# A Mamba-2 mixer with a mixture of experts: the count table stored step by step, the carry moved into a limit, the shared weights split during the mixer

## The chip, the cores and the metric

The kernel runs on one core of one Trainium2 chip. A core has a matrix engine (PE, with its weight loads shown apart as PEld), a vector engine (DVE), a scalar engine (ACT), GpSimd (POOL) and a sync engine (SP) that only issues DMAs. The engines run their own instruction lists and meet at semaphores. The metric is device time in microseconds, the median of several runs; lower is better. Everything is fp32.

## The reference

One block of a network over x of shape (2, 4096, 256), in two halves.

```
x = x + layernorm(mamba2(layernorm(x)))                  # the mixer
x = x + layernorm(moe(layernorm(x)))                     # the experts

moe(x):   T = 8192 tokens, E = 64 experts, top 8, capacity 128
  gu     = x @ shared_gate_up_w                          # (256, 1024)
  shared = silu(gu[:, :512]) * gu[:, 512:] @ shared_down_w
  shared = shared * sigmoid(x @ shared_gate_w)
  w, idx = top_k(softmax(x @ gate_w), 8);  w /= sum(w)
  pos    = how many earlier (token, choice) pairs took the same expert
  buf[e, slot] = x[token]     for slot = pos < 128
  out_e  = (silu(buf @ gate) * (buf @ up)) @ down        # per expert, 128 slots
  y      = sum over the token's choices of w * out_e[e, slot], 0 if pos >= 128
  return y + shared
```

Only the first 128 tokens (in order) that choose an expert reach it. So the kernel needs, per expert, a running count of choices over the 8192 tokens, and for each expert and slot 0..127 the token that sits there.

## The kernel before

**Mixer.** 32 steps; a step treats 128 tokens of both batches. The function `iteration(i)` of each engine is a software pipeline of depth 5: at `i` it works on parts of steps i, i-1, ... i-4 (`j0` to `j4`, and `j5`). Steps 0 to 6 and the last 8 are written out, the middle is a hardware loop. The order of the instructions on each engine is fixed by hand in these functions. In part `j4` PE multiplies the chosen-matrix by a triangle of ones into bank 1, and DVE adds the count so far (`count_now`, L1021) and writes 128 columns of `counts`, a tile of 128 partitions (64 experts times two batches) by 32 x 128 tokens; the two batches are counted apart. At `i + 1` DVE copies the last column into `count_now` (L830). SP loads x three steps ahead, stores the normed rows and router weights into the token table (L441, L446) and the transposed normed rows (L436). After three x loads SP also issues the zero fill of `routed_sum` (L423, L425). POOL starts each iteration with the small operations of the layernorm scale (L1034, then a power on L1027), and every tensor-tensor operation of POOL carries L1027, every one of DVE L807, every plain copy of ACT L665 here and L1523 in the experts' stage.

**Between the stages.** All engines wait for the mixer's stores, meet at a barrier, and SP clears the semaphores. The experts' stage then starts with a head. ACT issues the loads of the shared weights (L1525, L1526). PE moves the final count of batch 0 to the partitions of batch 1 (the carry); DVE keeps it (L1698), adds it to the 32 counts at step ends (L1700, `ends`), and compares those with 1..128 (`ends_before`, L1705, two halves); PE sums the comparisons (L1395), which gives for each expert and slot the step ("chunk") in which its token lies; DVE turns this into row numbers of the count table (L1709 to L1712). ACT adds the carry to the whole of `counts` (L1530), and only then SP stores it as the count table in HBM (L1261), with one row of 1..128 more (L1264). ACT writes a high part of the shared weights (L1532, L1534), DVE the rest (L1715, L1717), since the fp32 products there are made of three products of split parts. ACT and DVE wait for the table store before the loop.

**Experts' loop.** `iteration_r1` runs 16 rounds and drains: each round gathers count rows for four experts (POOL, indirect DMA, L1965 to L1983), compares them with `slot` (L1780 and on), which gives the token, gathers the tokens' rows, runs the experts, and adds the results into `routed_sum` by indirect DMA; in between PE makes the shared part from `xt` tiles that SP loads (L1275), ACT and DVE split (L1761, L1764). `row_now` holds the four row numbers of a round and is filled in two halves (L1738, L1767).

```
eng.wait_ge(carry_ready, 1)
eng.wait_ge(ends_kept, 1)
nc.scalar.activation(counts[:, :], counts[:, :], ACT.Identity, bias=carry).then_inc(counts_total, 1)
```

## Time and profile before

| | us |
|---|---|
| median of 3 runs | 1413.08 (1411.3 to 1415.54) |
| profiled execution, its own time | 1406.39 |
| span of its trace | 1404.7 |
| PE busy | 1225.8 (87%) |
| DVE busy | 1035.7 (74%) |
| POOL busy | 908.1 (65%) |
| ACT busy | 866.9 (62%) |

The span reaches from the first to the last instruction; 1.69 us of the execution lie around it. Busy shares are means over stages with different limits: the mixer until about 925, the head until about 946, the experts' loop and a last part that adds, normalises and stores.

### The profile page before, as it was taken

The numbers are of one execution on the slowest core, as the hardware profiler recorded it, in microseconds if no ns is written. First come the engines' busy times: TensorE is split into PE (matmuls) and PEld (weight loads), VectorE is DVE, ScalarE is ACT, GpSimd is POOL, SyncE is SP. The second block draws the span as 40 slices with busy tenths as digits, with TensorE's granted clock in tenths as the row PEclk, the third lists the DMA queues.
The fourth block names the chain that finished last, engine by engine and source line by source line (L and its number), as shares of the span: only waits on it lengthen the run. The fifth ranks groups of instructions, "written<-read, shape, count | busy, mean of one in ns | idle before, by whom it ended". The sixth has DMA issues, their size and how long they took to land. (4 is left out here: it accounts for less than half of the span.)

```text
span 1404.7 us, 27142 instructions
## 1 busy us (share of the span) xinstructions
PE 1225.8 (87%) x8578; PEld 1070.5 (76%) x8578; DVE 1035.7 (74%) x3118; ACT 866.9 (62%) x1882; POOL 908.1 (65%) x1049
## 2 busy tenths in 40 slices
PE   2899999999999999999999999729998999998960
PEld 2778778778777877877877787519998999998950
DVE  3789989998998999999899899544344344443894
ACT  2677777777777777777777777434444344444453
POOL 0466677667667767766766776516667677663586
PEclk9899999999999999999999999859999999999985
DMA  5600010011001001001100000156766676764565
GB/s 159 198 7 25 26 42 33 24 34 39 24 26 40 31 24 41 32 24 34 39 24 26 34 23 18 44 165 161 183 176 155 169 181 163 168 161 99 188 203 171
DMA packets 112935, 119.90 MB, mean 85 GB/s; under 512 B 19889, under 2 KB 99057, under 8 KB 112881
## 3 DMA queue, kind: packets, MB, share of 16 engines
q1 hardware_dynamic: 97744, 94.58, 21.4%
q0 software_dynamic: 14336, 23.08, 8.7%
q10 hardware_dynamic: 800, 1.57, 0.3%
q8 instruction: 27, 0.44, 0.1%
q14 instruction: 28, 0.22, 0.1%
HBM read 70.63 MB, written 48.56 MB: 85 GB/s over the span
## 5 line engine op out<-in xcount | busy, mean ns | idle before, releaser
L1027 POOL TENSOR_TENSOR mamba_arena<-mamba_arena 128x512 f32<-128x512 f32 (+2 forms) x384 | 383.3, 1009 | 245.0 <-DVE mamba_arena L807 199.4
L456 PE MATMUL bank<-identity,mamba_arena 128*128 128x128 f32 x704 | 112.5, 279 | 53.1 <-DVE mamba_arena L916 27.4
L807 DVE TENSOR_TENSOR mamba_arena<-bank,mamba_arena 128x512 f32<-128x512 f32 (+1 forms) x224 | 136.4, 610 | 15.9 <-PE bank L500 10.0
L456 PEld LDWEIGHTS bank<-identity,mamba_arena 128*128 128x128 f32 x704 | 85.0, 146 | 80.2 <-issue 27.2
L1378 PE MATMUL bank<-xt_hi,wsgu_hi 128*128 128x256 f32 x384 | 114.0, 297 | 17.2 <-DVE xt_lo L1761 13.8
L1378 PE MATMUL bank<-xt_lo,wsgu_hi 128*128 128x256 f32 x384 | 109.6, 285 | 0.0
L1378 PE MATMUL bank<-xt_hi,wsgu_lo 128*128 128x256 f32 x384 | 109.6, 285 | 0.0
L665 ACT ACTIVATE mamba_arena<-bank 128x512 f32<-128x512 f32 x192 | 100.4, 540 | 9.0 <-PE bank L456 6.6
L1378 PEld LDWEIGHTS bank<-xt_hi,wsgu_hi 128*128 128x128 f32 x384 | 74.6, 194 | 18.8 <-DVE xt_lo L1761 14.5
L807 DVE TENSOR_TENSOR mamba_arena<-bank_s,mamba_arena 128x1024 f32<-128x1024 f32 x64 | 77.9, 1217 | 3.5 <-ACT bank_s L705 2.2
L669 ACT ACTIVATE mamba_arena<-x_all,mamba_arena 128x256 f32 (+1 forms) x128 | 69.5, 594 | 12.1 <-DVE mamba_arena L853 7.3
L1378 PEld LDWEIGHTS bank<-xt_lo,wsgu_hi 128*128 128x128 f32 x384 | 74.6, 194 | 0.4
L1378 PEld LDWEIGHTS bank<-xt_hi,wsgu_lo 128*128 128x128 f32 x384 | 74.5, 194 | 0.0
L1027 POOL TENSOR_TENSOR mamba_arena<-mamba_arena,minus_half 128x2 f32<-128x2 f32 x96 | 68.4, 712 | 7.8
L596 PEld LDWEIGHTS bank<-mamba_arena 128*128 128x128 f32 x256 | 47.0, 193 | 30.7 <-ACT mamba_arena L757 17.8
L596 PE MATMUL bank<-mamba_arena 128*128 128x256 f32 x256 | 65.1, 398 | 0.6
L478 PEld LDWEIGHTS bank<-mamba_arena 128*128 128x128 f32 x256 | 48.5, 190 | 20.0 <-issue 14.9
L1027 POOL TENSOR_TENSOR run_moving<-run_t,head_of 64x1024 fp32r<-64x1024 f32 x32 | 60.6, 1892 | 4.4 <-ACT run_t L665 4.4
L565 PE MATMUL bank<-mamba_arena 128*128 128x64 f32 x512 | 60.8, 272 | 0.5 <-DVE mamba_arena L807 0.5
L500 PE MATMUL bank<-mamba_arena 128*128 128x64 f32 x512 | 61.0, 272 | 0.1
L478 PE MATMUL bank<-mamba_arena 128*128 128x256 f32 x256 | 60.6, 379 | 0.0
L565 PEld LDWEIGHTS bank<-mamba_arena 128*128 128x128 f32 x512 | 59.7, 192 | 0.7 <-DVE mamba_arena L807 0.7
(368 smaller groups left out, 4479.1 us busy)
## 6 DMA issues: line engine op xcount, KB each, us to landing
experts_arena<-in_egu SPq DMA_DIRECT2D x64, 256.0 KB, 3.7
routed_sum<-zeros SPq DMA_DIRECT2D x1, 8320.0 KB, 27.0
x_all<-in_x SPq DMA_DIRECT2D x32, 256.0 KB, 2.7
token_table<-mamba_arena SPq DMA_DIRECT2D x64, 128.0 KB, 1.7
normed_transposed<-mamba_arena SPq DMA_DIRECT2D x32, 256.0 KB, 2.1
experts_arena<-normed_transposed SPq DMA_DIRECT2D x32, 256.0 KB, 3.8
experts_arena<-in_edown SPq DMA_DIRECT2D x64, 128.0 KB, 3.0
experts_arena<-routed_sum SPq DMA_DIRECT2D x32, 256.0 KB, 3.4
```

Source lines behind the costliest of these rows:

```text
L456: return nc.tensor.transpose(out, in_, identity[:, :])
L478: last = nc.tensor.matmul(bank[0][:, 1 * DM:2 * DM], yt[:, 1, c, :], w_out[:, c, :], start=c == 0, stop=c == KI - 1)
L500: last = nc.tensor.matmul(bank[5][:, h * HD:(h + 1) * HD], decay[:, 0, h, :], xdt[:, 0, h, :], start=True, stop=True)
L565: last = nc.tensor.matmul(bank[2][:, h * HD:(h + 1) * HD], decay[:, 1, h, :], xdt[:, 1, h, :], start=True, stop=True)
L596: last = nc.tensor.matmul(bank[0][:, 0 * DM:1 * DM], yt[:, 0, c, :], w_out[:, c, :], start=c == 0, stop=c == KI - 1)
L665: return nc.scalar.activation(out, in_, ACT.Copy)
L669: last = nc.scalar.activation(out[:, b, :], x[b], ACT.Identity, bias=shift[:, b:b + 1], scale=scale[:, b:b + 1])
L807: return nc.vector.tensor_tensor(out, a, b, op)
L1027: return nc.gpsimd.tensor_tensor(out, a, b, op)
L1378: last = nc.tensor.matmul(out[:, f * 256:(f + 1) * 256], w[:, k, columns], x[:, k, :], start=n == 0, stop=n == len(parts) - 1)
```

## The change

Six edits.

1. `counts` shrinks to one step (128 x 128). Each step's counts go to the count table as soon as DVE has written them: SP issues two DMAs of 64 rows at the end of its iteration, behind the router weights. DVE waits, before it writes the next step's counts, for that store and for a copy of the last column that POOL now makes into `ends` (its first instruction of every iteration from i = 5).
2. The table therefore holds batch 1 without the carry. The comparison `count + carry <= slot` becomes `count <= slot - carry`: DVE computes once `limit`, per slot and expert, with the carry taken off where the chunk lies in batch 1 (four more small operations; PE adds one product that spreads the carries over the partitions), and each round copies four columns into `limit_now`.
3. The head loses ACT's addition over `counts`, the two large table stores and the waits on them.
4. The shared weights are loaded by SP in the mixer, behind the first three x loads and ahead of the zero fill, into slots of `x_all` that are used later. ACT writes the high part in six pieces of 128 x 512 in iterations 0 to 5 (the first waits for both loads), POOL subtracts for the rest in iterations 1 to 6.
5. `row_now` is filled at once, for round 0 already in the head.
6. `silu_s` and `act_s` get tiles of their own, since `counts` no longer has room for them.

```diff
-        counts = sb("counts", [P, STEPS * P])
+        counts = sb("counts", [P, P])
+        ends = sb("ends", [P, STEPS])
...
# SP, mixer
+                eng.dma_start(wsgu_raw, sgu_d.rearrange("(k p) f -> p k f", p=P)).then_inc(wsgu_loaded, 16)
+                eng.dma_start(wsdown_raw, sdown_d.rearrange("(k p) f -> p k f", p=P)).then_inc(wsdown_loaded, 16)
                 rows = (TOK + CAP) // P
...
+                    if real(j4):
+                        eng.wait_ge(counts_ready, j4 + 1)
+                        eng.nop(nofuse=True)
+                        for b in range(NB):
+                            eng.dma_start(counts_d[bass.ds(j4 * NE + b * STEPS * NE, NE), :], counts[b * NE:(b + 1) * NE, :]).then_inc(counts_stored, 16)
                 pipeline(eng, iteration)
+                eng.wait_ge(counts_stored, 32 * STEPS)
...
# ACT, mixer, behind the squares
+                    if is_number(i) and i < 6:
+                        if i == 0:
+                            eng.wait_ge(wsgu_loaded, 16)
+                            eng.wait_ge(wsdown_loaded, 16)
+                        copy(shared_piece(wsgu_hi, wsdown_hi, i), shared_piece(wsgu_raw, wsdown_raw, i)).then_inc(shared_high, 1)
...
# DVE, mixer
+                        if real(j4 - 1):
+                            eng.wait_ge(counts_stored, 32 * j4)
+                            eng.wait_ge(end_kept, j4)
+                        nc.vector.tensor_scalar(counts[:, :], bank[1][:, 0:P], count_now[:, :], None, ALU.add).then_inc(counts_ready, 1)
...
# POOL, mixer
+                    if real(j5):
+                        eng.wait_ge(counts_ready, j5 + 1)
+                        eng.nop(nofuse=True)
+                        nc.gpsimd.tensor_copy(ends[:, bass.ds(j5, 1)], counts[:, P - 1:P]).then_inc(end_kept, 1)
...
+                    if is_number(i) and 0 < i < 7:
+                        eng.wait_ge(shared_high, i)
+                        tt(shared_piece(wsgu_lo, wsdown_lo, i - 1), shared_piece(wsgu_raw, wsdown_raw, i - 1),
+                           plain(shared_piece(wsgu_hi, wsdown_hi, i - 1)), ALU.subtract)
...
# SP, experts
-                eng.wait_ge(counts_total, 1)
-                for b in range(NB):
-                    eng.dma_start(counts_v[:, b * STEPS:(b + 1) * STEPS, :],
-                                  counts[b * NE:(b + 1) * NE, :].rearrange("e (i t) -> e i t", t=P)).then_inc(tables_out, 16)
...
# ACT, experts
-                nc.scalar.activation(counts[:, :], counts[:, :], ACT.Identity, bias=carry).then_inc(counts_total, 1)
-                eng.wait_ge(wsgu_loaded, 16)
-                nc.scalar.activation(wsgu_hi[:, :, :], wsgu_raw, ACT.Copy).then_inc(sgu_split[0], 1)
-                eng.wait_ge(wsdown_loaded, 16)
-                nc.scalar.activation(wsdown_hi[:, :, :], wsdown_raw, ACT.Copy).then_inc(sdown_split[0], 1)
-                eng.wait_ge(tables_out, 16 * 3)
...
# DVE, experts, head and round
+                nc.vector.scalar_tensor_tensor(row_of[:, :], chunk_of, float(NE), expert, ALU.mult, ALU.add).then_inc(row_ready, 1)
+                eng.wait_ge(row_ready, 1)
+                nc.vector.tensor_copy(row_now[:, :], row_of[:, 0:4]).then_inc(row_now_ready, 1)
...
+                nc.vector.tensor_tensor(limit, late, spread_bank, ALU.mult).then_inc(late_carry, 1)
+                eng.wait_ge(late_carry, 1)
+                nc.vector.tensor_scalar(limit, limit, -1.0, slot, ALU.mult, ALU.add).then_inc(limit_ready, 1)
...
-                        nc.vector.tensor_scalar(below[:, 0, 0, :], slot_counts[:, 0, 0, :], slot, None, ALU.is_le, ALU.add,
+                        nc.vector.tensor_scalar(below[:, 0, 0, :], slot_counts[:, 0, 0, :], limit_now[:, 0:1], None, ALU.is_le, ALU.add,
```

The first place is DVE in the head, from the sum of the comparisons to the first split of an `xt` tile. In brackets stand the semaphores waited for; those of the last rows bear names of the mixer, whose numbers they reuse. Before:

```order
L1709 COPY experts_arena<-bank 128x64 [waits chunks_counted]
L1711 TENSOR_SCALAR experts_arena<-experts_arena 128x64 [waits chunks_kept]
L1712 SCALAR_TENSOR_TENSOR row_of<-experts_arena 128x64
L1715 TENSOR_TENSOR wsgu_lo<-experts_arena,wsgu_hi 128x2048 [waits sgu_split0]
L1717 TENSOR_TENSOR wsdown_lo<-experts_arena,wsdown_hi 128x1024 [waits sdown_split0]
L1738 COPY row_now<-row_of 128x2 [waits row_ready,tables_out]
L1761 TENSOR_TENSOR xt_lo<-experts_arena,xt_hi 128x512 [waits o_scale]
```

And in the changed kernel:

```order
L1725 COPY experts_arena<-bank 128x64 [waits chunks_counted]
L1727 SCALAR_TENSOR_TENSOR row_of<-experts_arena 128x64 [waits chunks_kept]
L1729 COPY row_now<-row_of 128x4 [waits row_ready]
L1730 TENSOR_SCALAR experts_arena<-experts_arena 128x64
L1731 TENSOR_SCALAR experts_arena<-experts_arena 128x64
L1733 SCALAR_TENSOR_TENSOR experts_arena<-experts_arena 128x64 [waits late_from]
L1735 TENSOR_TENSOR experts_arena<-experts_arena,bank 128x64 [waits late_only]
L1737 TENSOR_SCALAR experts_arena<-experts_arena 128x64 [waits late_carry]
L1758 COPY experts_arena<-experts_arena 128x4 [waits limit_ready]
L1781 TENSOR_TENSOR xt_lo<-experts_arena,xt_hi 128x512 [waits x2_ready]
```

The two wide subtractions and the wait on the table are gone; `row_now` stands two operations behind the sum, and five small operations on 64 columns and a copy stand before the split.

The second place is SP in the mixer's loop, from the rows' store to the loop's end, before:

```order
L441 ISA [waits x2_normed]
L441 DMA token_table<-mamba_arena 128x256
L441 ISA
L441 DMA token_table<-mamba_arena 128x256
L446 ISA [waits weights_ready]
L446 DMA token_table<-mamba_arena 128x64
L446 ISA
L446 DMA token_table<-mamba_arena 128x64
L406 REGISTER_ALU
L406 COMPARE_AND_BRANCH
```

And the end of the same loop in the changed kernel:

```order
L460 ISA [waits weights_ready]
L460 DMA token_table<-mamba_arena 128x64
L460 ISA
L460 DMA token_table<-mamba_arena 128x64
L465 ISA [waits counts_ready]
L465 DMA count_table<-counts 64x128
L465 ISA
L465 DMA count_table<-counts 64x128
L418 REGISTER_ALU
L418 COMPARE_AND_BRANCH
```

Two issues and a wait on DVE are added behind the last store of the iteration, ahead of the next x load.

The third is the start of POOL's loop, in the changed kernel:

```order
L1062 ISA [waits counts_ready]
L1062 COPY ends<-counts 128x1
L1064 REGISTER_ALU
L1066 TENSOR_SCALAR mamba_arena<-mamba_arena 128x2 [waits x_mean]
L1055 TENSOR_TENSOR mamba_arena<-mamba_arena,minus_half 128x2 [waits x_var]
```

The last two rows are those with which the loop began before; the first three are new.

## Rows read from the trace of the kernel before

**Rows 1.** Stretches: us, busy PE, PEld, DVE, ACT, POOL, PE clock, DMA share, GB/s.
```profile
422.00:827.00 405.00, 385.43 (x2564) 320.11 (x2563) 369.34 (x1066) 301.18 (x631) 281.66 (x360) 1.00 0.09 31
925.00:944.00 19.00, 2.65 (x34) 2.25 (x34) 9.29 (x13) 7.74 (x4) 0.48 (x3) 0.50 0.81 211
```

**Rows 2.** Chain that ended last, over the head: start, us, what.
```profile
925.30 0.43 ACTq L1525
...
927.58 3.72 ACT counts L1530
...
931.31 0.66 SPq L1261
...
932.03 2.33 SPq L1261
...
934.41 5.08 SPq L1264
...
939.52 5.18 DMA experts_arena<-normed_transposed
```

**Rows 3.** DVE's timeline in the head: start, us, instruction [idle before, releaser].
```profile
926.78 4.49 DVE L1705 TENSOR_TENSOR experts_arena<-experts_arena 128x2048 bf16<-128x2048 f32 x2
932.40 0.23 DVE L1709 COPY experts_arena<-bank 128x64 f32<-128x64 f32 x1 [1.13 <-PE bank L1395]
...
932.77 0.22 DVE L1712 SCALAR_TENSOR_TENSOR row_of<-experts_arena 128x64 uint32<-128x64 f32 x1
```

**Rows 4.** Timeline of all engines at the start of the loop.
```profile
943.91 0.17 DVE L1738 COPY row_now<-row_of 128x2 uint32<-128x2 uint32 x1 [7.37 <-issue]
...
944.79 0.63 ACT L1523 ACTIVATE xt_hi<-experts_arena 128x512 fp32r<-128x512 f32 x1 [10.76 <-DMA experts_arena<-normed_transposed]
944.98 1.24 POOL L1965 DMA_INDIRECT experts_arena<-count_table,row_now  x1 [19.17 <-DVE row_now L1738]
945.45 0.69 DVE L1761 TENSOR_TENSOR xt_lo<-experts_arena,xt_hi 128x512 fp32r<-128x512 f32 x1 [1.37 <-ACT xt_hi L1523]
```

**Rows 5.** SP's timeline: the last issue of the mixer.
```profile
922.37 0.81 SPq L446 DMA_DIRECT2D token_table<-mamba_arena  x2
```

**Rows 6.** Timeline of all engines in the drain, iteration 34.
```profile
910.59 0.32 DVE L1021 TENSOR_SCALAR counts<-bank,count_now 128x128 f32<-128x128 f32 x1
910.83 0.22 POOL L1042 TENSOR_SCALAR mamba_arena<-mamba_arena 128x2 f32<-128x2 f32 x1 [0.61 <-DVE mamba_arena L1013]
...
912.13 1.09 ACT L669 ACTIVATE mamba_arena<-x_all,mamba_arena 128x256 f32<-128x256 f32 x2 [3.23 <-DVE mamba_arena L853]
```

**Rows 7.** Timeline of all engines in iteration 0.
```profile
25.66 0.62 SPq L423 DMA_DIRECT2D routed_sum<-zeros  x1
...
31.67 0.22 ACT L720 ACTIVATE mamba_arena<-mamba_arena 128x16 f32<-128x16 f32 x1 [1.29 <-DVE mamba_arena L903]
...
32.34 0.16 DVE L911 TENSOR_SCALAR mamba_arena<-mamba_arena 128x16 f32<-128x16 f32 x1
```

**Rows 8.** DMA issues: count, KB each, median us from issue to landing.
```profile
count_table<-counts SPq DMA_DIRECT2D x2, 1024.0 KB, 9.0
...
experts_arena<-in_sdown ACTq DMA_DIRECT2D x1, 512.0 KB, 6.1
```

**Rows 9.** DVE's waits from 400 to 805: us in total, times, longest.
```profile
DVE xnt_lo L807 <- ACT xnt_hi L665: 11.1, 15, 0.8
...
DVE mamba_arena L849 <- PE bank L478: 3.7, 15, 0.3
```

**Rows 10.** Timeline at the turn of two iterations of the mixer's loop.
```profile
420.50 1.04 POOL L1027 TENSOR_TENSOR mamba_arena<-mamba_arena 128x512 f32<-128x512 f32 x1 [1.17 <-DVE mamba_arena L807]
...
421.61 0.66 DVE L807 TENSOR_TENSOR mamba_arena<-mamba_arena 128x512 f32<-128x512 f32 x1
421.86 0.49 POOL L1034 TENSOR_SCALAR mamba_arena<-mamba_arena 128x2 f32<-128x2 f32 x1 [0.31 <-DVE mamba_arena L821]
```

**Rows 11.** POOL's timeline, iteration 3, at the place of a new piece.
```profile
104.50 1.29 POOL L1027 TENSOR_TENSOR mamba_arena<-mamba_arena 128x512 f32<-128x512 f32 x1 [1.00 <-DVE mamba_arena L807]
```

More of the change, by code:

```diff
@@ L105, in build @@
         x_all = sb("x_all", [P, NB, STEPS, DM])
-        counts = sb("counts", [P, STEPS * P])
+        counts = sb("counts", [P, P])
+        ends = sb("ends", [P, STEPS])
+        wsgu_hi, wsgu_lo = (sb(f"wsgu_{part}", [P, KD, 2 * FS], F32R) for part in ("hi", "lo"))
+        wsdown_hi, wsdown_lo = (sb(f"wsdown_{part}", [P, FS // P, DM], F32R) for part in ("hi", "lo"))
         shared_tanh = sb("shared_tanh", [P, NB, STEPS])
@@ L392, in real, with shared_piece @@
             return not is_number(j) or 0 <= j < STEPS
+        def shared_piece(gate_up, down, c):
+            return gate_up[:, c // 2, (c % 2) * FS:(c % 2 + 1) * FS] if c < 4 else down[:, 2 * (c - 4):2 * (c - 4) + 2, :].rearrange("p k d -> p (k d)")
         def draining(i):
@@ L829, in iteration @@
                         eng.nop(nofuse=True)
-                        nc.vector.tensor_copy(count_now[:, :], counts[:, bass.ds(j5 * P + (P - 1), 1)])
+                        nc.vector.tensor_copy(count_now[:, :], counts[:, P - 1:P])
                     if real(j1):
@@ L1125, in build @@
         shared = view(NB, STEPS // 2, DM)
-        wsgu_raw = shared[:, 1, 0:KD * 2 * FS // DM, :].rearrange("p (k a) d -> p k (a d)", k=KD)
-        wsdown_raw = shared[:, 1, KD * 2 * FS // DM:][:, 0:FS // P, :]
-        ends = view(STEPS)
+        carry_spread, late = shared[:, 1, 0, 0:NE], shared[:, 1, 0, NE:2 * NE]
         ends_before = (shared[:, 0, 0:STEPS * P // (2 * DM), :].rearrange("p a d -> p (a d)").bitcast(BF16)
@@ L1137, in build @@
         slot = view(1)
+        limit = view(NE)
+        limit_now = view(2 * 2)
         expert = view(NE)
@@ L1394, in _ @@
                         eng.wait_ge(ends_compared, 1 if i == 0 else 2)
-                    last = nc.tensor.matmul(chunk_bank[:, 0:NE], ends_before[:, i, :], fold, start=i == 0, stop=i == STEPS - 1)
+                    last = nc.tensor.matmul(chunk_bank, ends_before[:, i, :], fold, start=i == 0, stop=i == STEPS - 1)
                 last.then_inc(chunks_counted, 1)
@@ L1694, in _ @@
                 nc.vector.memset(carry_from[:, 0:NE], 0.0)
-                nc.vector.tensor_copy(carry_from[:, NE:P], identity[:, 0:NE]).then_inc(carry_matrix, 1)
+                nc.vector.tensor_copy(carry_from[:, NE:P], identity[:, 0:NE])
+                nc.vector.tensor_scalar(carry_spread[0:NE, :], identity[0:NE, 0:NE], count_now[0:NE, :], None, ALU.mult).then_inc(carry_matrix, 1)
                 nc.vector.tensor_tensor(fold, identity[:, 0:NE], identity[:, NE:P], ALU.add)
                 eng.wait_ge(carry_moved, 1)
-                nc.vector.tensor_copy(carry, carry_bank[:, 0:1]).then_inc(carry_ready, 1)
+                nc.vector.tensor_copy(carry, carry_bank).then_inc(carry_ready, 1)
                 eng.wait_ge(carry_ready, 1)
-                nc.vector.tensor_scalar(ends, counts[:, P - 1::P], carry, None, ALU.add).then_inc(ends_kept, 1)
+                nc.vector.tensor_scalar(ends[:, :], ends[:, :], carry, None, ALU.add).then_inc(ends_kept, 1)
                 eng.wait_ge(ends_kept, 1)
@@ L1737, in iteration_r1 @@
                         eng.nop(nofuse=True)
-                        nc.vector.tensor_copy(row_now[:, 0, :], row_of[:, bass.ds(4 * j0 + 0, 2)]).then_inc(row_now0, 1)
+                        if not is_number(j0) or j0 > 0:
+                            nc.vector.tensor_copy(row_now[:, :], row_of[:, bass.ds(4 * j0, 4)]).then_inc(row_now_ready, 1)
+                        nc.vector.tensor_copy(limit_now, limit[:, bass.ds(4 * j0, 4)]).then_inc(limits_now, 1)
                     if real(j1, 16):
@@ L1783, in iteration_r1 @@
                         eng.wait_ge(counts_gathered01, 16 * j0 + 16)
-                        nc.vector.tensor_scalar(below[:, 0, 1, :], slot_counts[:, 0, 1, :], slot, None, ALU.is_le, ALU.add,
+                        nc.vector.tensor_scalar(below[:, 0, 1, :], slot_counts[:, 0, 1, :], limit_now[:, 1:2], None, ALU.is_le, ALU.add,
                                                 accum_out=offset[:, 0, 1:2]).then_inc(offset_ready01, 1)
@@ L1806, in iteration_r1 @@
                         eng.wait_ge(counts_gathered10, 16 * j0 + 16)
-                        nc.vector.tensor_scalar(below[:, 1, 0, :], slot_counts[:, 1, 0, :], slot, None, ALU.is_le, ALU.add,
+                        nc.vector.tensor_scalar(below[:, 1, 0, :], slot_counts[:, 1, 0, :], limit_now[:, 2:3], None, ALU.is_le, ALU.add,
                                                 accum_out=offset[:, 1, 0:1])
@@ L1810, in iteration_r1 @@
                         eng.wait_ge(counts_gathered11, 16 * j0 + 16)
-                        nc.vector.tensor_scalar(below[:, 1, 1, :], slot_counts[:, 1, 1, :], slot, None, ALU.is_le, ALU.add,
+                        nc.vector.tensor_scalar(below[:, 1, 1, :], slot_counts[:, 1, 1, :], limit_now[:, 3:4], None, ALU.is_le, ALU.add,
                                                 accum_out=offset[:, 1, 1:2]).then_inc(offset_ready11, 1)
```

70 lines of the change are left out of this document (29 added, 41 removed).

## The prediction

> **What bounds the kernel now.** I read the stretches first, to see which stage has a hole. In the mixer's loop PE is busy for 385 of 405 us at full clock: a bound by PE, with DVE close behind, where little can be won. Between 925 and 944 PE is busy for 2.65 of 19 us and its granted clock is at the lower level, 0.50 [rows 1]. Then the chain of waits, to see what holds that hole open: ACT's pass over `counts` (3.72 us), two table stores on SP's queue (0.66 and 2.33), the small store behind them, which sits 5.08 in a full queue, and then the load of the first `xt` tile, 5.18 [rows 2]. Last the timelines of the single engines there: DVE is done with the row numbers at 932.99 (932.77 + 0.22) and fills `row_now` only at 943.91 [rows 3, 4], held by the wait on the table. So one chain, count table first and everything else behind it, sets the start of the experts' loop. The shared weights are not what ends last.
>
> **The head of the experts' stage.** I count from its start, 925.30 [rows 2], and call that 0. Before, the two events that start the loop are POOL's first gather of count rows at 19.7 (944.98) and the end of the first split of `xt` at 20.8 (945.45 + 0.69) [rows 4].
>
> Removed from that chain: 3.72 + 0.66 + 2.33 + 5.08 = 11.8 us of it. What is late next is DVE. It begins its comparisons at 1.5, they take 4.49 and PE's sum ends at 7.1, where DVE copies it (932.40) [rows 3]; none of this changes, but for one small operation and one small product ahead of it, which I set at 0.1. Then:
> - copy 0.23 and row numbers 0.22 end at 7.65, the fill of `row_now` (0.17) at 7.8. POOL began its gather 0.9 after that copy's end before (944.08 to 944.98) [rows 3, 4], so now at 8.7: 11.0 earlier.
> - the rest of `limit` and the copies are six operations, each about 0.22 by the row-number operation and partly waiting for its forerunner: 1.3 us, so DVE is free at 9.1. The `xt` tile is issued by SP behind one small store at about 1.5, lands with the 5.18 of before at 6.7, and ACT has its high part at 7.4 (0.63) [rows 2, 4]: ready before DVE is. The split ends at 9.1 + 0.7 = 9.8: 11.0 earlier.
>
> Both events move by the same amount, so the loop starts 11.0 earlier whichever of them is the one that matters. Bounds: 11.8 if the six operations hide beside the gather's flight, 9.5 if the tile's load or the row numbers take 1.5 longer because all of it now runs close together. Inside the rounds one copy of DVE goes and one comes; POOL's third gather no longer waits for the second half of `row_now`. I count both at nothing.
>
> **The end of the mixer.** SP issues two more DMAs behind the last pair. A pair takes 0.81 [rows 5], and the barrier follows the landing of the last one as before: +0.8. It can't be less, since nothing else runs there. In the drain POOL now begins an iteration by waiting for the counts of the one before. In iteration 34 its first operation started at 910.83, while the counts are written until 910.91 [rows 6]; copy (about 0.2) and wait put it at about 911.2, and ACT, which had been idle for 3.23 us, waits for that line: +0.4. In iterations 33 and 35 the same delay ends in longer waits.
>
> **The beginning.** SP issues the two weight loads at 25.66, where the zero fill stood [rows 7], so the second at about 26.1. On ACT's queue the pair took up to 6.1 us [rows 8]; it lands at about 32.2. ACT waits for both ahead of the exponential of iteration 0, which started at 31.67 [rows 7]; with the piece (0.63 [rows 4]) in front it starts at 32.9 and DVE's next dependent operation moves from 32.34 [rows 7] to 33.3. From there DVE is busy without gaps to the end of this iteration's convolution, so nothing gives it back: +1.0. Bounds: 0.3 if the loads land at 31.5, 3.8 if they take 9.0 as the table stores did [rows 8]. I take 1.1. The zero fill and the next x loads go later by the weights' time, and no one needs them for tens of us.
>
> The Trainium skill, page "DMA: Bandwidth & Descriptors", section "Anatomy of one DMA — SWDGE (gpsimd) path", fits a DMA as about 2.0 us plus its bytes at 436 GB/s. An estimate from it is 5.6 us for both loads, against the 6.1 measured here for one of a pair; the start would then cost 0.6 and the sum be half a microsecond better.
>
> **The steady mixer.** Three things are added. ACT's pieces in iterations 1 to 5 stand ahead of an exponential for which ACT waits anyway. POOL's pieces in 1 to 6 take 1.04 us each [rows 10] where POOL waits for DVE; the smallest such wait in these six is 1.00 [rows 11]. SP's two issues end about 1 us later than its iteration did, and its x load is three steps ahead. The one addition in every step is POOL's copy at the head. POOL is free from 421.54 to 421.86 there [rows 10], so the copy's 0.2 fits if it starts at once. If it does not, the line behind it moves by up to 0.3, then DVE's shift, and what takes that up are two waits of DVE right behind it: 3.7 / 15 = 0.25 for PE and 11.1 / 15 = 0.74 for ACT [rows 9]. So: 0 per step, with 0.1 as the upper end of the forecast, which is 2.7 over 27 steps. DVE's two new waits are for things done a whole step earlier.
>
> A gain in a step is excluded: nothing leaves the path there.
>
> A row shows that POOL's small operation takes 0.49 us beside a DVE operation of 0.66 on SBUF operands [rows 10]. The Trainium skill, page "SBUF — State Buffer", section "SBUF: two separate sides", says that the two engines lock one port pair for a whole instruction when DVE has two SBUF inputs. By that rule the copy would either wait for DVE's operation or hold it back; the trace agrees in that the 0.49 end with DVE's operation. This is the mechanism of the slower rival below.
>
> **Sum.** -11.0 + 0.8 + 0.4 + 1.1 + 0 = -8.7 us, against the span of 1404.7 and the profiled execution's 1406.39: 1397.7 for a profiled one. The runs of before have their median 6.7 above that execution, and I carry the difference over: 1413.1 - 8.7 = 1404.4, 0.6% less.
>
> **Rivals.**
> - *Larger gain.* The first exponential is hardly delayed, the six operations hide, and POOL's third gather of an early round comes forward. -11.8 + 0.8 + 0.4 + 0.3 = -10.3, with a microsecond from the gather -11.3: 1402. For it: POOL and its indirect DMAs are long on the chain in the loop. Against it: the experts' rounds keep PE busy too, and a gather that comes earlier only waits for it. 0.10.
> - *Small prices add up.* The loads take 9.0 (+2.7 more), each step costs 0.1 (+2.7): -3.3, 1409.8. For it: the first wait has no cover at all, and the zero fill stands on the same queue. Against it: it stands behind. 0.15.
> - *The gain is given back in the loop.* If the loop's end hangs on something that does not start with it, only the prices stay: +2.3, 1415.4. Against it: all that the chain names in the loop (scatters, gathers, PE) starts from the two events above. 0.07.
> - *The lock in every step, slower.* POOL's copy comes to lie against DVE's 0.66 us operation in the turn of each iteration, the two scale operations behind it slip past the covers of 0.25 and 0.74, and PE, whose transposes need the normed rows, waits. The price is then about half a microsecond a step, one more hold of the kind in [rows 10]: 27 x 0.5 = 13.5, less 8.7 is +4.8, 1417.9. For it: PE is 95% busy there [rows 1], and every delay that reaches it counts 27 times. Against it: both covers stand right behind the place. It cancels the gain from 0.32 a step. 0.06.
>
> **How the numbers follow.** The forecast has 0.62, with a range of its own of 1401.5 to 1407.5 (its bounds of 11.8 and 9.5, of 0.3 and 3.8, and up to 0.1 a step, not all at once). The range of 1400 to 1411 takes in the larger gain and the small prices; what is left out is the loop, the lock and the tails. About 0.3%, 4.2 us, is what a measurement here can tell from no change. Faster: the forecast but for a little of its upper tail, and the larger gain, 0.73. Same: the small prices, the gain given back, and that tail: 0.21. Slower: 0.06, the lock.
>
> **What would show it.** The time from the first instruction of the head to the first split of `xt` should shrink from 20.2 us (925.30 to 945.45) to about 9.1. The chain there should run over DVE's comparisons and PE's sum, with no ACT pass and no SP queue. POOL's first gather should come 8.7 after the head's start. The head's start itself should come about 2.3 later than 925.3. In iteration 0 the exponential should wait for a DMA until about 32.9. The period of the mixer's loop should be what it was, with DVE's waits of 0.25 and 0.74 a little shorter. The prediction is wrong if that period is longer by more than 0.17, if the head's events are not both about 11 earlier, or if the loop takes longer from first gather to last scatter.

## The result

| | us |
|---|---|
| before, median of 11 runs | 1413.07 (1407.53 to 1417.52) |
| changed, median of 11 runs | 1405.81 (1400.74 to 1409.58) |
| ratio to before | 0.9957, 95% interval 0.9946 to 0.9968 |
| changed, profiled execution and its span | 1404.88, 1403.2 |
| forecast | 1404.4 (1400 to 1411) |

The change is faster by 4.5 to 7.6 us, by the ratio's interval on 1413: 0.4%. The median lies 1.4 above the forecast. The two profiled executions differ by only 1.5 us, because that of before was 6.7 below its kernel's median and that of the changed kernel 0.9 below its own. So no stage is judged here by the ends of two traces. In all 14 traces were taken, four of them of the kernel before, and stages are compared among them.

**The profile after: the head.** The stretches that answer to [rows 1], of the changed kernel (us, busy PE, PEld, DVE, ACT, POOL, PE clock, DMA share, GB/s):

```profile
425.00:830.00 405.00, 385.34 (x2564) 319.99 (x2563) 369.25 (x1066) 301.08 (x631) 283.46 (x375) 1.00 0.11 33
930.00:949.00 19.00, 12.04 (x98) 11.53 (x99) 10.22 (x30) 3.31 (x5) 6.45 (x9) 0.65 0.47 147
```

The mixer's loop reads as before. Of the 19 us at the head PE is busy for 12.04 where it was for 2.65. (Each window starts just ahead of the head of its own trace.) Its chain (start, us, what), against [rows 2]:

```profile
931.99 4.50 DVE experts_arena L1721 x2
936.49 0.05 issue
936.54 1.05 PE bank L1425 x16
937.58 0.02 issue
937.61 0.24 DVE experts_arena L1725
937.85 0.02 issue
937.87 0.24 DVE row_of L1727
938.10 0.02 issue
938.13 0.18 DVE row_now L1729
938.31 0.03 POOLq L1982
938.34 0.91 issue
939.25 1.24 POOL experts_arena L1983
```

ACT's pass and SP's queue are gone, and DVE's comparisons, PE's sum and the row numbers hold the chain. The timeline of all engines, against [rows 3, 4]:

```profile
930.50 0.11 DVE L1709 MEMSET experts_arena<- 128x64 f32 x1 [4.43 <-PEq L90]
...
934.43 0.63 ACT L1549 ACTIVATE xt_hi<-experts_arena 128x512 fp32r<-128x512 f32 x1 [2.73 <-DMA experts_arena<-normed_transposed]
...
938.13 0.17 DVE L1729 COPY row_now<-row_of 128x4 uint32<-128x4 uint32 x1
...
939.25 1.24 POOL L1983 DMA_INDIRECT experts_arena<-count_table,row_now  x1 [8.32 <-DVE row_now L1729]
939.40 0.17 DVE L1758 COPY experts_arena<-experts_arena 128x4 f32<-128x4 f32 x1
939.48 0.69 DVE L1781 TENSOR_TENSOR xt_lo<-experts_arena,xt_hi 128x512 fp32r<-128x512 f32 x1
```

Counted from DVE's first instruction, the first gather comes at 8.75 (19.59 before) and the first split ends at 9.67 (20.75). ACT had the high part of the `xt` tile ready at 935.06 (934.43 + 0.63), 4.4 us before DVE began its split: DVE is what is late, as forecast.

**The end of the mixer.** SP's timeline, against [rows 5], and the drain's iteration 34, against [rows 6]:

```profile
926.13 0.81 SPq L460 DMA_DIRECT2D token_table<-mamba_arena  x2
927.04 1.11 SPq L465 DMA_DIRECT2D count_table<-counts  x2
```

```profile
913.83 0.35 DVE L1049 TENSOR_SCALAR counts<-bank,count_now 128x128 f32<-128x128 f32 x1
...
914.31 0.18 POOL L1062 COPY ends<-counts 128x1 f32<-128x1 f32 x1 [0.85 <-DVE counts L1049]
...
914.58 0.22 POOL L1074 TENSOR_SCALAR mamba_arena<-mamba_arena 128x2 f32<-128x2 f32 x1
...
915.90 1.09 ACT L689 ACTIVATE mamba_arena<-x_all,mamba_arena 128x256 f32<-128x256 f32 x2 [3.75 <-DVE mamba_arena L878]
```

From the last weights' store to the head's first DVE instruction it is 4.37 us (before 925.39 - 922.37 = 3.02): 1.35 more, of which 1.21 lies between the end of the pair's issue (926.94) and that of the new pair (928.15). In iteration 34 ACT's wait grew from 3.23 to 3.75: half a microsecond.

**The beginning.** ACT's timeline in iteration 0, against [rows 7]:

```profile
32.94 0.63 ACT L685 ACTIVATE wsgu_hi<-x_all 128x512 fp32r<-128x512 f32 x1 [2.79 <-DMA x_all<-in_sdown]
33.48 0.20 ACT L745 ACTIVATE mamba_arena<-mamba_arena 128x16 f32<-128x16 f32 x1
```

The second load was issued at 26.00 and took 6.8 us. The exponential starts at 33.48; the forecast had 32.9. In the next iteration, behind its exponential at 59.50, there is something that the prediction had not priced. These are stretches (columns as above), first of the kernel before, then of the changed one:

```profile
62.00:75.00 13.00, 12.45 (x64) 8.97 (x65) 11.53 (x28) 10.64 (x20) 7.25 (x7) 1.00 0.01 3
```

```profile
62.00:75.00 13.00, 12.38 (x69) 9.61 (x69) 10.48 (x32) 8.50 (x18) 4.88 (x5) 0.87 0.10 35
```

PE's granted clock fell to its lower level (1.2 GHz of 2.4) for 3 to 4 us from 66.0 on. PE's timelines there show the price in one group, first before and then after:

```profile
64.32 1.03 PE L589 MATMUL bank<-mamba_arena 128*128 128x512 f32 x2
```

```profile
66.16 1.92 PE L609 MATMUL bank<-mamba_arena 128*128 128x512 f32 x2
```

**The steady mixer.** The turn of two iterations, against [rows 10], and DVE's waits from 403 to 808, against [rows 9]:

```profile
424.45 0.19 POOL L1062 COPY ends<-counts 128x1 f32 x1
424.57 0.66 DVE L832 TENSOR_TENSOR mamba_arena<-mamba_arena 128x512 f32<-128x512 f32 x1
...
424.82 0.49 POOL L1066 TENSOR_SCALAR mamba_arena<-mamba_arena 128x2 f32<-128x2 f32 x1 [0.18 <-DVE mamba_arena L846]
```

```profile
DVE xnt_lo L832 <- ACT xnt_hi L685: 11.1, 15, 0.7
...
DVE mamba_arena L874 <- PE bank L498: 3.8, 15, 0.3
```

POOL's copy takes 0.19 and still leaves a wait of 0.18 behind it. Both of DVE's waits are what they were, within 0.1 us of the totals. SP's next x load comes 1.6 us later in the iteration (425.62, and 421.08 before, with the whole trace 2.97 later here); the forecast had about 1, and nothing waits for it. The period, from ACT's exponentials of iterations 8 and 27, is (761.24 - 247.89) / 19 = 27.018, and before (758.26 - 244.91) / 19 = 27.018.

### The profile page after: what moved, and what is told of

Its sections match the earlier page's. It is cut to its first block and busy times, and to the rows that moved or that the text cites. A ratio compares the mean times of both kernels' runs of the same rounds, so it can differ in the third digit from the quotient of the medians.

```text
span 1403.2 us, 27454 instructions
## 1 busy us (share of the span) xinstructions
PE 1229.4 (88%) x8580; PEld 1072.8 (76%) x8580; DVE 1033.4 (74%) x3121; ACT 863.0 (62%) x1885; POOL 919.8 (66%) x1087
```

## The experiments

Each kernel is the changed one with the edit shown, unless it says otherwise. What all traces have in common is set out here once. "Exp. 5" is the start of ACT's exponential in iteration 5. "Low clock" adds up, over stretches of 1 us from 26 to 200, the time that PE had the lower level. "Gather" is from the head's start (DVE's memset) to POOL's first gather, "loop" from the start of that gather to the start of the last scatter. (The expectations of the first two experiments give 345.3 and 348.2 for the loop: those count to the last scatter but one.) The medians are not all on one scale, because each group of kernels had its own runs of before beside it: their median was 1410.90 for piece_end and weights_in_head, 1410.84 for head_delayed, two_halves and piece_and_stores, and 1412.91 for pieces_late and late_and_stores. Compare the ratios; they differ by up to 0.001 from the quotients of these medians.

| kernel of the trace | exp. 5 | low clock | head's start | gather | loop | execution |
|---|---|---|---|---|---|---|
| before | 163.49 | 10.2 | 925.39 | 19.59 | 349.85 | 1406.39 |
| before_again | 163.32 | 6.8 | 925.13 | 19.62 | 349.90 | 1408.20 |
| before_third | 164.09 | 10.2 | 926.64 | 19.73 | 350.55 | 1409.77 |
| before_fourth | 163.30 | 10.2 | 925.22 | 19.62 | 355.93 | 1412.58 |
| changed | 166.58 | 13.6 | 930.50 | 8.75 | 352.78 | 1404.88 |
| after_again | 164.85 | 10.2 | 929.70 | 8.76 | 353.71 | 1403.45 |
| piece_end | 164.01 | 6.8 | 928.05 | 8.75 | 351.69 | 1401.52 |
| weights_in_head | 163.32 | 10.2 | 928.32 | 8.74 | 356.12 | 1405.98 |
| head_delayed | 166.93 | 17.1 | 931.28 | 20.38 | 351.48 | 1416.05 |
| two_halves | 167.58 | 17.1 | 931.61 | 8.75 | 351.80 | 1404.91 |
| piece_and_stores | 166.39 | 17.1 | 930.75 | 8.75 | 353.52 | 1406.03 |
| three_copies | 167.65 | 17.1 | 932.97 | 8.75 | 351.44 | 1404.54 |
| pieces_late | 163.30 | 10.2 | 928.10 | 8.75 | 353.03 | 1402.79 |
| late_and_stores | 165.70 | 13.7 | 929.34 | 8.75 | 351.04 | 1401.08 |

### Both kernels once more

> The kernel before, unchanged, for a second trace of it. In the first one the stretch from POOL's first gather of counts to its last scatter took 345.3 us, in the changed kernel 348.2. Theory (the experts' loop varies from execution to execution): this trace has 345 to 350, and the mixer up to the head starts within 1 us of 925.3. Rival (the changed loop is systematically 3 us longer): this trace has 345 again, within 1 us. The head from its start to the first gather is 19.7 and to the end of the first split 20.8 for both.

> The changed kernel, unchanged, for a second trace of it. Theory: the head is fixed work, so gather at 8.8 and end of the split at 9.7 after the head's start, again within 0.2; the period of the mixer's loop 27.02 again; from iteration 0 on the start costs 1.6 us (the exponential at 33.5), and the 1.5 more that the first trace showed between 62 and 72 us, where PE's clock fell to its lower level for about 3 us, is a matter of chance: it may be gone here (head's start at 929.0 instead of 930.4). Rival: the dip of the clock belongs to the changed start and comes again. Loop from first gather to last scatter: 345 to 350 by the theory, 348 by the rival of a longer loop.

Measured: the head repeated to 0.03 us in both. The start of the changed kernel was 1.7 us cheaper this time (164.85), without the second fall of the clock. The loop of before took 349.90 again and that of the changed kernel 353.71. In after_again the last exponential (iteration 31) came 1.3 later than those ahead of it, behind a fall of PE's clock at 846.6; weights_in_head below has the same at 845.4, and none of the four traces of before has it. Two traces each spoke for a loop that had become 3 to 4 us longer, so this rival was taken up below.

### ACT's first piece at the end of iteration 0

```diff
-                    if is_number(i) and i < 6:
-                        if i == 0:
-                            eng.wait_ge(wsgu_loaded, 16)
-                            eng.wait_ge(wsdown_loaded, 16)
+                    if is_number(i) and 0 < i < 6:
...
+                    if is_number(i) and i == 0:      # end of the iteration
+                        eng.wait_ge(wsgu_loaded, 16)
+                        eng.wait_ge(wsdown_loaded, 16)
+                        copy(shared_piece(wsgu_hi, wsdown_hi, 0), shared_piece(wsgu_raw, wsdown_raw, 0)).then_inc(shared_high, 1)
```

> The first weight piece of ACT and its two waits stand at the end of iteration 0 instead of ahead of the exponential. Theory (the wait for the weights has no cover and all of the start's cost hangs on it): the exponential comes at 31.7 again, the offsets against the kernel before in iteration 3 fall from +3.3 to within 0.3 of zero, the head starts 2 to 3 us earlier than in the changed kernel, and the time is 1403.3, ratio to the kernel before 0.993 to 0.995. Rival (the cost of the start is the clock of PE and the transfers, not the wait): the exponential comes early but the offset in iteration 3 stays at 1.5 or more, ratio 0.9957 as with the change.

Measured: 1402.79 median of 7, ratio 0.9953 (0.9934 to 0.9972), which can't be told from the changed kernel's 0.9957. The exponential of iteration 0 came at 32.67, not at 31.7. That of iteration 3 came at 110.03, 0.85 before the cheaper of the two changed traces and still 0.75 to 0.9 behind the two traces of before that were there then; the two taken later have it at 109.88 and 109.11. So the theory's fall to within 0.3 did not come against three of four traces, but before itself varies by 0.8 there. Whether what is left (0.7 on the mean) sits in the pieces of iterations 1 to 5 is not shown.

### The count table alone: the weights back in the head

```diff
-                eng.dma_start(wsgu_raw, ...)              # SP, mixer; likewise wsdown_raw
-                        copy(shared_piece(...))           # ACT, iterations 0 to 5
-                        tt(shared_piece(...))             # POOL, iterations 1 to 6
+                nc.scalar.activation(wsgu_hi[:, :, :], wsgu_raw, ACT.Copy).then_inc(sgu_split[0], 1)      # ACT, head
+                nc.vector.tensor_tensor(wsgu_lo[:, :, :], wsgu_raw, plain(wsgu_hi[:, :, :]), ALU.subtract).then_inc(sgu_split[1], 1)  # DVE, behind the limit
```

(and the same two operations for `wsdown`, with ACT issuing both loads in the head, and the waits of PE and ACT for the split parts)

> The count table, the ends and the limit as in the changed kernel; the shared weights are loaded and split in the head as before (ACT 1.9 and 1.0, DVE 2.3 and 1.2 behind the limit). Theory (the count table is what held the head open, and the weights' move is worth only the 3.5 us of DVE in the head less the cost of the start): no cost in iteration 0 (exponential at 31.7), gather 8.8 after the head's start as in the changed kernel, end of the first split at 13.3 instead of 9.7; the time lies between 1403 and 1407, ratio 0.993 to 0.996. Rival A (the loop starts from the split, so all of the 3.5 counts and the start is cheap): 1408 to 1410, ratio 0.997. Rival B (the loop starts from the gathers alone): the weights' place costs nothing, 1403, ratio 0.993.

Measured: 1403.56 median of 12, ratio 0.9955 (0.9941 to 0.9969), the same as the whole change. The start cost nothing (163.32), and DVE's timeline in the head shows what came back:

```profile
937.15 2.29 DVE L1740 TENSOR_TENSOR wsgu_lo<-experts_arena,wsgu_hi 128x2048 fp32r<-128x2048 f32 x1
939.36 1.22 DVE L1742 TENSOR_TENSOR wsdown_lo<-experts_arena,wsdown_hi 128x1024 fp32r<-128x1024 f32 x1
...
940.56 0.69 DVE L1785 TENSOR_TENSOR xt_lo<-experts_arena,xt_hi 128x512 fp32r<-128x512 f32 x1
```

The first split ended at 12.9 after the head's start instead of 9.7. So moving the weights takes 3.3 us from the head's split and costs about 3 at the start. All of the gain that can be measured is the count table's; the move as it was made adds none. Rival A's 0.997 and rival B's 0.993 lie outside the interval, each by little. Whether the loop starts from the gather or from the split is therefore not settled.

### The head made as long as before

```diff
+                for n, half in enumerate((0, 1, 0, 1, 0)):
+                    chunks = slice(half * STEPS // 2, (half + 1) * STEPS // 2)
+                    nc.vector.tensor_tensor(ends_before[:, chunks, :], ...).then_inc(delayed, 1)   # the comparison, once more
+                    eng.wait_ge(delayed, n + 1)
                 for half in range(2):
```

> The changed kernel with five more halves of the comparison on DVE ahead of the real two: the head is longer by 5 x 2.24 = 11.2 us, so that the first gather and the first split come as late after the head's start as in the kernel before (about +20 and +21). So far the mean gap between two scatters was 5.20 and 5.18 us in two traces of the kernel before and 5.24 to 5.28 in four of changed ones; over 63 gaps that is 4 to 5 us. Theory A (earliness: the head is no longer what the loop waits for alone, so part of its gain is given back in the first rounds): the mean gap falls back to 5.18 to 5.20, the last scatter moves later by only 7 to 8 us, and the time is 7 to 8 us above the changed kernel's, ratio to the kernel before about 1.001. Theory B (the code of the rounds is what is slower, by one fill for two and the limit's copy): the gap stays at 5.24 to 5.28, the last scatter moves by the whole 11.2, ratio 1.0037.

Measured: 1416.93 median of 12, ratio 1.0037 (1.0021 to 1.0054). Over the changed kernel's 0.9957 that is 0.0080, or 11.3 us, for a delay of 11.6 by the trace (gather at 20.38 instead of 8.75):

```profile
932.77 11.60 DVE L1722 TENSOR_TENSOR experts_arena<-ends,experts_arena 128x2048 bf16<-128x2048 f32 x5
```

The two intervals together leave the 11.3 uncertain by about 3 us. So a microsecond in the head is about a microsecond at the end. Theory A's ratio of 1.001 lies outside the interval: a loss of 3 to 4 us of the head's gain in the loop is refuted. Theory B had the right number too, but the mean gap between scatters, 5.245, does not tell it from chance.

### Two halves of row_now again

```diff
-                            nc.vector.tensor_copy(row_now[:, :], row_of[:, bass.ds(4 * j0, 4)]).then_inc(row_now_ready, 1)
+                            nc.vector.tensor_copy(row_now[:, 0:2], row_of[:, bass.ds(4 * j0, 2)]).then_inc(row_now_ready, 1)
...
+                        nc.vector.tensor_copy(row_now[:, 2:4], row_of[:, bass.ds(4 * j0 + 2, 2)]).then_inc(row_now1, 1)
...
+                        eng.wait_ge(row_now1, j0 + 1)      # POOL, third gather
```

> The changed kernel, but row_now is filled in two halves again at the two old places of DVE's round, and POOL waits for the second half ahead of its third gather of counts. Theory B (the single fill lets POOL issue its third gather earlier, which puts the scatters behind it later): mean gap of the scatters 5.19 and the time 4 us below the changed kernel's, ratio 0.993. Theory A (earliness): no difference, gap 5.24 to 5.28, ratio 0.9955.

Measured: 1404.24 median of 11, ratio 0.9951 (0.9935 to 0.9967), loop 351.80. Theory B's 0.993 lies outside the interval. How `row_now` is filled makes no difference that can be measured.

### Two more traces of the kernel before

> The kernel before, for a third trace. In the first two, POOL's first gather to its last scatter took 349.9 us, in seven traces of changed kernels 351.4 to 353.7 (and 356.1 with the weights in the head). But the delayed head passed on its 11.2 us in full, so nothing of the head's gain seems lost in the loop. Theory C (chance: the two traces were of executions 3 and 7 us shorter than their kernel's median): this one has 351 to 354. Theory B (the changed rounds are slower): 350 again. PE at the lower clock between 26 and 200 us: 7 to 10 us in all, as in the first two.

> The kernel before, for a fourth trace, for the same question: gather to last scatter 351 to 354 by theory C, 350 by theory B; PE at the lower clock for 7 to 10 us between 26 and 200 us, with no second fall after 60 us.

Measured: loops of 350.55 and 355.93. The four of before now span 349.85 to 355.93 (mean 351.6), nine changed ones without the weights in the head 351.04 to 353.71 (mean 352.3). The third trace fitted theory B, and the fourth lies above even theory C's 354: the same kernel varies by 6 us in the loop. The difference of the means, 0.7, is far inside that spread, so the traces show no longer loop, and they can't exclude one of a microsecond or more either.

### Three copies on POOL

```diff
+                        nc.gpsimd.tensor_copy(spare0[:, bass.ds(j5, 1)], counts[:, P - 1:P])
+                        nc.gpsimd.tensor_copy(spare1[:, bass.ds(j5, 1)], counts[:, P - 1:P])
                         nc.gpsimd.tensor_copy(ends[:, bass.ds(j5, 1)], counts[:, P - 1:P]).then_inc(end_kept, 1)
```

> The changed kernel with two more copies of the same column (to spare columns) at POOL's start of each iteration: 3 small copies of about 0.19 us instead of one. The period of the mixer's loop is 27.02 us with none and with one. Theory (POOL's slack of 0.31 ahead of its scale operation and the waits of 0.25 and 0.74 behind it take up a delay of some 0.4): the period stays within 0.1 of 27.02. Rival (a copy that lies against DVE's operations holds them back, and one was just covered): 27.3 to 27.5, 8 to 13 us on the whole.

Measured: a period of (762.49 - 248.98) / 19 = 27.027. SP's timeline shows it too, and those of POOL and DVE show the copies:

```profile
425.00 1.18 SPq L466 DMA_DIRECT2D count_table<-counts  x2
...
452.02 1.18 SPq L466 DMA_DIRECT2D count_table<-counts  x2
```

```profile
425.70 0.71 POOL L1064 COPY spare<-counts 128x1 f32 x1
425.70 0.67 DVE L833 TENSOR_TENSOR mamba_arena<-mamba_arena 128x512 f32<-128x512 f32 x1
426.35 0.18 POOL L1065 COPY ends<-counts 128x1 f32 x1
426.61 0.22 POOL L1069 TENSOR_SCALAR mamba_arena<-mamba_arena 128x2 f32<-128x2 f32 x1
```

The second copy starts with DVE's operation on SBUF operands and takes 0.71 us, as long as that operation, where the others take 0.18; it does so in all 20 steps from 250 to 800 us. DVE's own operation takes 0.66 or 0.67, as ever. So the copy that was held is POOL's, and the work behind it comes 0.4 us later. DVE's waits from 404 to 809 show what takes this up:

```profile
DVE mamba_arena L862 <- POOL mamba_arena L1056: 9.7, 15, 0.7
DVE xnt_lo L833 <- ACT xnt_hi L686: 5.3, 15, 0.4
```

The wait for POOL grew from 3.9 to 9.7 (0.26 to 0.65 a step), and the wait for ACT behind it shrank from 11.1 to 5.3 (0.74 to 0.35). The period of 27.027 can't be told from that of the kernels with one copy, 27.018 to 27.026 where nothing else was changed in the mixer. The prediction's slower rival needed 0.3 to 0.5 a step; with one copy all of the 0.74 is still there.

### The first piece later, and the last stores on ACT

```diff
-                    if real(j4):
+                    if real(j4) and not (is_number(j4) and j4 == STEPS - 1):      # SP
...
+                eng.wait_ge(counts_ready, STEPS)                                   # ACT, behind the last tanh
+                for b in range(NB):
+                    eng.dma_start(counts_d[bass.ds((STEPS - 1) * NE + b * STEPS * NE, NE), :], counts[b * NE:(b + 1) * NE, :]).then_inc(counts_stored, 16)
```

(with the edit of piece_end)

> The changed kernel with ACT's first weight piece at the end of iteration 0, and the last step's two count stores issued by ACT behind its last tanh instead of by SP behind the weights. The first edit made the exponential of iteration 3 come 0.9 us earlier than in the undisturbed trace of the changed kernel. The second should take 0.9 to 1.1 us from the stretch between the last exponential and the head (60.5 us with the change, 58.7 before), since ACT and SP then end their issues within 0.3 us of each other. Together 2 us, 1403.5 on the scale of the first comparison, ratio 0.994. Rival (the landing of the last stores, not their issue, holds the barrier, and it takes longer from two queues): the stretch stays at 60.5 and the ratio at 0.9955.

Measured: 1405.13 median of 10, ratio 0.9951 (0.9934 to 0.9969). From the weights' store to the head's start it is 930.75 - 927.18 = 3.57 instead of 4.37: 0.8 won. The whole stretch from the last exponential to the head was 60.9, not 59.5, because the weights' store itself came 1.3 later after that exponential than in after_again (57.32 against 56.05); three_copies, without this edit, has 57.42 there, so the edit is not the reason, and the traces do not say what is. The start had a second fall of the clock again (17.1 us of low clock), although the first piece stood at the end of iteration 0. So that edit does not prevent it.

### The pieces after the start

```diff
-            for i in range(DEPTH_1 + 2):
+            for i in range(DEPTH_1 + 9):       # iterations written out
...
-                    if is_number(i) and i < 6:
+                    if is_number(i) and 7 <= i < 13:      # ACT, piece i - 7, the waits at i == 7
...
-                    if is_number(i) and 0 < i < 7:
+                    if is_number(i) and 7 < i < 14:       # POOL, piece i - 8
```

> The changed kernel with fourteen iterations of the mixer written out instead of seven, so that ACT can write the six pieces in iterations 7 to 12 and POOL subtract in 8 to 13; the loads stay where they are. With the change PE spent 10 to 17 us at the lower clock between 26 and 200 us, 13.6 or more in five of six traces with the pieces in iterations 0 to 6, against 7 to 10 without moved weights. Theory (the wait for the loads and the pieces beside the filling pipeline make PE's holes longer, and its clock falls again): 7 to 10 us of low clock, the exponential of iteration 5 at 163.4 to 164 instead of 166.7 on average, head's start 3 us earlier, time 1402.5 on the first scale, ratio 0.993. Rival (it is the transfers of 1.5 MB): the low clock stays at 13 us or more and the ratio at 0.9955.

> The same and the last step's count stores issued by ACT, which gave 0.8 us between the last weights' store and the head's start in one trace (3.6 instead of 4.4 us). If both add up: 1401.7 on the first scale, ratio 0.9925, a little faster than any kernel here. Rival: as pieces_late or, if its theory falls, as the changed kernel, 0.995.

Measured: pieces_late 1399.92 median of 6, ratio 0.9904 (0.9884 to 0.9925); with the last stores on ACT 1400.51, ratio 0.9914 (0.9896 to 0.9933). Both are faster than the changed kernel, whose interval ends at 0.9946. In pieces_late the start is that of before: exponential of iteration 5 at 163.30, 10.2 us of low clock, and the stretch that showed the fall of the clock reads

```profile
62.00:75.00 13.00, 12.59 (x65) 9.09 (x65) 11.58 (x27) 10.78 (x20) 7.39 (x7) 1.00 0.10 32
```

although the same transfers run (0.10 of the DMA engines, 32 GB/s, as in the changed kernel). In late_and_stores, with the same start, the exponential of iteration 1 was already 1.2 later than in pieces_late (58.85 and 57.61), the clock then fell again at 65.4, and exponential 5 came at 165.70. Where the pieces now stand they are not free: from the exponential of iteration 7 to that of iteration 15 both kernels lose 0.9 us against before. The edit also writes out seven more iterations of the mixer, and no kernel has that alone, so the 0.9 and the gain are those of both together. The last stores kept what they had won; SP, then ACT, then DVE:

```profile
925.76 1.04 SPq L460 DMA_DIRECT2D token_table<-mamba_arena  x2
```

```profile
925.48 1.23 ACTq L830 DMA_DIRECT2D count_table<-counts  x2
```

```profile
929.34 0.11 DVE L1712 MEMSET experts_arena<- 128x64 f32 x1 [3.64 <-PEq L90]
```

Against the changed kernel the head starts 3.1 us earlier in pieces_late (928.10 against a mean of 931.2 over changed, after_again, head_delayed, two_halves and three_copies). The times say about 6 (1399.92 against 1405.81, with before at 1412.91 and 1413.07). The traced execution of pieces_late was the slowest of its six, 2.9 above their median, and that of the changed kernel was 0.9 below its own: the two traces differ by only 2.1 in time. So the traces can show no more than that, and in which stage the rest of the 6 lies stays open.

## Why the prediction was right, and where it was off

**The chain at the head: right.** Forecast gather at 8.7 and split at 9.8 after the head's start; measured 8.75 and 9.67, 10.8 and 11.1 earlier than in the first trace of before (10.9 for the gather by all four). The late next was DVE, as said. The tile, forecast to land at 6.7, was with ACT at 3.9 already, which changes nothing.

**The loop passes it on: right, and now shown** by head_delayed, not only argued: 11.3 us at the end (give or take 3) for 11.6 in the head. The rival of a gain given back is refuted.

**The two stores at the end: 0.8 forecast, 1.35 measured.** The pair was priced by the pair before it (0.81); it took 1.11 and came 0.1 behind.

**The drain: 0.4 forecast, 0.5 measured**, at the line that was named.

**The steady mixer: 0, and 0.** The period is equal to the third decimal. The hold that the slower rival spoke of exists: in three_copies a copy takes 0.71 us beside DVE's 0.67. But the 0.4 that two more copies bring ends in the cover that the prediction had named against it, DVE's wait of 0.74 for ACT, of which 0.35 is still left. The Trainium skill states a lock of a shared port pair, held for a whole instruction, between GpSimd and a DVE operation with two SBUF inputs, on the page "SBUF — State Buffer", section "SBUF: two separate sides"; the trace agrees with it by the 0.71 of that copy.

**The start: the term that was mis-sized.** The prediction put down 1.1, from a wait that it placed at 32.2 (it ended at 32.94; by its own working its bounds of 0.3 and 3.8 should read 0.5 and 4.0), and held the pieces of iterations 1 to 6 for hidden, each beside a wait. The second load took 6.8 us. The fit of the Trainium skill, page "DMA: Bandwidth & Descriptors", section "Anatomy of one DMA — SWDGE (gpsimd) path", had made 5.6 of both as an estimate. The trace does not agree with that; the page's fit is for DMAs issued by GpSimd, and SP issued these. Measured at iteration 5, over five traces with the pieces as changed, it is 166.7 (164.85 to 167.65) against 163.55 (163.30 to 164.09) of before: 3.2. In the cheapest, after_again, 1.3 of it stands alone; in the others PE's clock fell a second time. That happened between 60 and 200 us in none of five traces without moved weights, in five of seven with pieces in the first iterations, and in one of two with only the loads there. That the move brings it on is thus likely; which part of the move does, pieces or loads, the runs don't settle, and the falls at 845.4 in weights_in_head, whose weights are not moved, and at 846.6 in after_again show that the pieces are not the only thing that can. A bound of 3.8 had been given for another reason (slow loads), so the range held, but the mechanism was not in the prediction.

**The sum.** -10.9 + 1.35 + 0.5 + 3.2 + 0 = -5.9, and the ratio says -6.1 (-4.5 to -7.6). One part of the mixer is missing from that sum: between the exponential of iteration 5 and the last one the five traces of these pieces take 0.5 us more than before on the mean, 1.3 in after_again and 0.15 to 0.4 in the others. With it the head starts 5.6 later than before on the mean of those traces (931.2 and 925.6), and the sum is -5.3, still in the interval. The forecast of -8.7 was 2.8 to 3.4 too good by its stages. That its time came within 1.4 us owes something to the median, which says -7.3; that part is luck.

**Signs that had been named.** The head's start was to come 2.3 later and came 5.1 later: most of the difference is the start's term again. A loop longer from first gather to last scatter was named as a sign of being wrong, and the first pair of traces showed it (352.78 and 349.85). Four traces of before from 349.85 to 355.93 then showed that one pair can't be read that way.

## What to carry to other kernels

Work moved out of an exposed stage into the start of a pipeline is not free merely because each piece finds an idle engine. Here PE's clock fell once more in five of seven traces with the pieces in the first iterations, and the two kernels that had them seven iterations later (with those iterations written out) had ratios of 0.9904 and 0.9914 instead of 0.9957. Look at the granted clock as well as at the waits. Price an edit on its own: here one half made all of the gain that could be measured, and the other none where it first stood. Before two traces are read as a change of a stage, take a third and a fourth of the same kernel.

## What was not expected of the hardware

- The loop of the experts, in one and the same program, took 349.85 to 355.93 us in four executions of the kernel before.
- PE's clock fell a second time, for 3 to 7 us, at 65 to 67, 89 to 90 or 115 us, in traces of nearly the same instructions, at 1.1 to 2.3 us each: from the exponential of iteration 1 to that of 2 it was 26.95 us in late_and_stores and 27.34 in the changed kernel instead of 25.80, from 2 to 3 in piece_and_stores 28.0 instead of 25.75, and from 3 to 5 in head_delayed 56.3 instead of 54.2.
- A 128x1 copy on POOL took 0.71 us when it started with a DVE operation of 0.67 with two inputs in SBUF, and 0.18 otherwise (three_copies, in every step); the DVE operation was not slower.
- Issuing took longer where SP and ACT did it at the same time: in both traces with the last stores on ACT, SP's pair of small stores took 1.04 us to issue where it took 0.81 alone, and ACT's pair 1.23 where SP's took 1.11.
